# Key stacks moved with their zeros in 1 KB pieces, query rows in 512-byte pieces, and one wait fewer ahead of the stacks

## The reference, cut to what matters

```python
q = (layernorm(x) @ Wq.T + bq)          # 128 sequences, 64 tokens, 16 heads of 8
k, v = (ctx @ Wk.T + bk), (ctx @ Wv.T + bv)
scores = einsum('bhqd,bhkd->bhqk', q, k) / sqrt(8)
x = x + (softmax(scores) @ v) @ Wo.T + bo
z = layernorm(x)
# two gates: convolution over 4 channels, batch norm over all tokens, GELU, linear, softmax, top 32 of 128
x = x + (z @ W) * top32(gate_out) + (z * top32(gate_in)) @ W + bias
```

## Time and profile before

| | us |
|---|---|
| median of 3 runs | 524.53 |
| lowest, highest | 522.14, 526.05 |
| the profiled execution | 522.13 |
| its span | 520.3 |

### The profile page before, as it was taken

How to read it: one execution, slowest core, us unless ns; L and a number is a source line. 1 busy time by engine, 2 the same in 40 slices (tenths; PEclk the granted TensorE clock), 3 DMA queues, 4 the chain that set the end, 5 groups by cost and what they waited for, 6 DMA issues and landing times.

```text
span 520.3 us, 16344 instructions
## 1 busy us (share of the span) xinstructions
PE 414.4 (80%) x5516; PEld 314.0 (60%) x5516; DVE 408.7 (79%) x1940; ACT 391.4 (75%) x1061; POOL 363.5 (70%) x515
## 2 busy tenths in 40 slices
PE   3457999989999989999989564987787877777754
PEld 1125787868877858887777242765564645555543
DVE  7554478766777766767875359999999999999997
ACT  3414677867787858887667488899989898899893
POOL 7356667776777767876311023699989898999896
PEclk9997799988999999999999855578879698788687
DMA  5788788788788787788810000000000000000001
GB/s 159 157 211 196 159 197 196 197 204 195 172 183 184 191 195 176 161 185 182 178 47 7 1 0 2 1 21 23 21 22 37 12 36 22 21 21 22 23 21 40
DMA packets 138970, 53.02 MB, mean 102 GB/s; under 512 B 105146, under 2 KB 131195, under 8 KB 137339
## 3 DMA queue, kind: packets, MB, share of 16 engines
q1 hardware_dynamic: 136712, 51.47, 41.2%
q10 hardware_dynamic: 2176, 0.52, 0.5%
HBM read 34.67 MB, written 16.78 MB: 99 GB/s over the span
## 4 chain that ended last, share of the span: by engine, by line
DVE 37%; SPq 27%; PE 18%; DMA 7%; issue 4%; ACT 4%; POOL 2%; DVEq 0%; ACTq 0%; POOLq 0%
SPq L300 23%; DVE kst L1040 17%; DVE tops L1033 16%; DMA k_scratch<-k_parts 4%; PE ps_pv L360 4%; DMA qst<-q_scratch 3%; PE ps_col L345 2%; SPq L285 2%; PE ps_row L389 2%; PE ps_mix L375 1%; PE ps_proj L437 1%; SPq L247 1%; PE ps_proj L415 1%; PE ps_turn L430 1%; PE ps_mix L604 1%
## 5 line engine op out<-in xcount | busy, mean ns | idle before, releaser
L892 DVE TENSOR_REDUCE m<-ps_row 128x8 f32<-128x512 f32 x128 | 82.3, 686 | 57.1 <-PE ps_row L389 56.9
L650 ACT ACTIVATE pT<-ps_col 128x512 f32<-128x512 f32 x128 | 68.7, 589 | 29.1 <-PE ps_col L345 28.9
L1033 DVE MAX8 tops<-kst 128x8 f32<-128x128 f32 x384 | 78.1, 268 | 0.0
L360 PE MATMUL ps_pv<-vx,pT 128*64 128x18 f32 x2048 | 73.3, 214 | 0.0
L360 PEld LDWEIGHTS ps_pv<-vx,pT 128*64 128x64 f32 x2048 | 66.9, 141 | 7.1 <-issue 4.5
L1040 DVE MATCH_REPLACE8 kst<-tops,kst 128x128 f32<-128x128 f32 x264 | 69.0, 266 | 0.0
L389 PE MATMUL ps_row<-kst,qst 96*64 96x128 bf16 x1024 | 42.7, 228 | 7.8 <-DMA qst<-q_scratch 7.7
L345 PEld LDWEIGHTS ps_col<-qst,kst 100*128 100x128 bf16 x1024 | 35.0, 100 | 22.8 <-issue 11.9
L345 PE MATMUL ps_col<-qst,kst 100*128 100x64 bf16 x1024 | 42.8, 197 | 5.9 <-DMA qst<-mT 5.7
L553 PE MATMUL ps_proj<-wf_sb,x2T 128*128 128x128 f32 x128 | 25.6, 362 | 26.2 <-ACT x2T L821 26.2
L389 PEld LDWEIGHTS ps_row<-kst,qst 96*64 96x64 bf16 x1024 | 33.5, 116 | 11.8 <-DMA qst<-q_scratch 9.9
(11 more groups left out here) (156 smaller groups left out, 1213.3 us busy)
## 6 DMA issues: line engine op xcount, KB each, us to landing
k_scratch<-k_parts SPq DMA_DIRECT2D x32, 192.0 KB, 3.0
q_scratch<-q_parts SPq DMA_DIRECT2D x32, 192.0 KB, 3.1
kst<-k_scratch SPq DMA_DIRECT2D x32, 192.0 KB
qst<-q_scratch SPq DMA_DIRECT2D x32, 192.0 KB
xr<-in_x_dram SPq DMA_DIRECT2D x16, 256.0 KB, 4.3
cT<-in_ctxT_dram SPq DMA_DIRECT2D x16, 256.0 KB, 3.6
kst<-k_scratch SPq DMA_DIRECT2D x32, 128.0 KB
qst<-q_scratch SPq DMA_DIRECT2D x32, 128.0 KB
```

The lines of the kernel that those rows point to most:

```text
L360: mm = pe.matmul(pv_flat[pp * SEQ:(pp + 1) * SEQ, h * 2 * VW:(h + 1) * 2 * VW], pT[:, 2 * j + pp, hh, :], vx[s][:, 2 * hp + pp, h, :], sta ...
L650: act.activation(pT[:, b % PT_RING, :, :], ps_col[b % 2][:, :, :], ACT.Exp, scale=SCALE).then_inc(act_exp, 1)
L892: dve.tensor_reduce(m32[:, b // 4, :, 4 * j:4 * j + 4].rearrange("q a h -> q h a"), ps_row[b % 2][:, :, :, :], AX.X, ALU.max).then_inc(dve ...
L1033: ins = dve.max(tops[g % 2][:, n, 8 * rnd:8 * rnd + 8], source(g, rnd, n))
```

## The change

The key parts get a new home, `k_frames`: each part of a pair lies as 64 values of the sequence and 64 zeros. It is zeroed once by VectorE, and GpSimd writes only the places of the values. The parts go to DRAM with the zeros (pieces of 1 KB in place of 512 bytes), and come back so into the stack: a row is 16 pieces of 1 KB in place of 64 of 128 bytes. The three stack buffers are therefore no longer zeroed. In DRAM a row of either scratch tensor is followed by a gap of 32 values; by that a query row is 16 pieces of 512 bytes. The stacks' wait for `act_mT` is gone.

```diff
+GAP = 32
...
-        k_parts = sb("k_parts", [128, PARTS, GTOK], BF16)
+        k_frames = sb("k_frames", [128, 2 * (PARTS * GTOK + SEQ)], BF16)
...
-        q_scratch = [nc.dram_tensor(f"q_scratch{s}", (2, PARTS, 128, HALF), BF16).ap() for s in range(2)]
-        k_scratch = [nc.dram_tensor(f"k_scratch{s}", (2, PARTS, 128, HALF), BF16).ap() for s in range(2)]
+        q_scratch = [nc.dram_tensor(f"q_scratch{s}", (2, PARTS, 128, HALF + GAP), BF16).ap() for s in range(2)]
+        k_scratch = [nc.dram_tensor(f"k_scratch{s}", (2, PARTS, 128, GTOK + GAP), BF16).ap() for s in range(2)]
+        k_parts = [k_frames[:, :].rearrange("c (a x) -> c a x", a=2)[:, :, n * GTOK:(n + 1) * GTOK]
+                   .rearrange("c a (p m) -> c a p m", p=PAIRS)[:, :, :, 0:SEQ] for n in range(PARTS)]
...
             for s in range(STACKS):
-                if s == 1:
-                    sp.wait_ge(gp_zero, 1)
-                else:
-                    sp.wait_ge(dve_zero, s // 2 + 1)
-                if s == 2:
-                    load_x(2)
                 sp.dma_start(kst[s][MROWS:KROWS, :, :, :, :].rearrange("r h p a m -> r (h p a m)"), minus_rows).then_inc(rows_in, 16)
+            load_x(2)
...
+                for a in range(2):
+                    sp.dma_start(k_scratch[s][a, :, :, 0:GTOK].rearrange("n c t -> c n t"),
+                                 k_frames[:, a * PARTS * GTOK:(a + 1) * PARTS * GTOK].rearrange("c (n t) -> c n t", n=PARTS)
+                                 ).then_inc(k_out[s], 16)
...
-                        src = scratch[s][a, first:first + n].rearrange("n (i h) t -> (n i) (h t)", h=HEADS)
-                        rows = spread(a, n)
-                        dst = (kst[d][rows, :, :, a, :].rearrange("r h p m -> r (h p) m") if to_keys
-                               else qst[d][rows, :, :].rearrange("r h t -> r (h t)"))
-                        if to_keys:
-                            src = src.rearrange("r (x m) -> r x m", m=SEQ)
-                        sp.dma_start(dst, src).then_inc(moved[d], 16)
+                        src = scratch[s][a, first:first + n].rearrange("n (i h) t -> (n i) h t", h=HEADS)
+                        sp.dma_start(stacks[d][spread(a, n)], src[:, :, 0:stacks[d].shape[2]]).then_inc(moved[d], 16)
...
-                    wait(sp, act_mT, 2 * t)
                     wait(sp, pe_col, 8 * (t - 1))
...
-            dve.memset(kst[0][:, :, :, :, :].bitcast(F32).rearrange("r h p a m -> r (h p a m)"), 0.0).then_inc(dve_zero, 1)
+            dve.memset(k_frames[:, :].bitcast(F32), 0.0).then_inc(dve_zero, 1)
...
-                    dve.memset(kst[2][:, :, :, :, :].bitcast(F32).rearrange("r h p a m -> r (h p a m)"), 0.0).then_inc(dve_zero, 1)
...
-            pool.memset(kst[1][:, :, :, :, :].bitcast(F32).rearrange("r h p a m -> r (h p a m)"), 0.0).then_inc(gp_zero, 1)
```

More of the change, by code:

```diff
@@ L264, in _, with write_keys @@
             for s in range(STACKS):
[L266 to L271 removed]
                 sp.dma_start(kst[s][MROWS:KROWS, :, :, :, :].rearrange("r h p a m -> r (h p a m)"), minus_rows).then_inc(rows_in, 16)
[L274 removed]
+            load_x(2)
+            def write_keys(g):
                 s = g % 2
[L276 to L280, removed]
+                wait(sp, gp_split, 4 * g + 4)
@@ L281, in write_parts @@
                 if g >= 2:
-                    wait(sp, moved[slot(g - 2)], STACK * uses(g - 2))
+                    wait(sp, k_moved[slot(g - 2)], STACK * uses(g - 2))
                 for a in range(2):
-                    sp.dma_start(scratch[s][a].rearrange("n c t -> c n t"),
-                                 parts[:, :, a * HALF:(a + 1) * HALF]).then_inc(done[s], 16)
-            def stack(g, scratch, done, moved, to_keys):
+                    sp.dma_start(k_scratch[s][a, :, :, 0:GTOK].rearrange("n c t -> c n t"),
+                                 k_frames[:, a * PARTS * GTOK:(a + 1) * PARTS * GTOK].rearrange("c (n t) -> c n t", n=PARTS)
+                                 ).then_inc(k_out[s], 16)
@@ new lines, in write_queries, with stack @@
+            def write_queries(g):
+                s = g % 2
+                wait(sp, dve_split, 4 * min(g + 1, 2))
+                wait(sp, gp_qsplit, 4 * (g - 1))
+                if g >= 2:
+                    wait(sp, q_moved[slot(g - 2)], STACK * uses(g - 2))
+                for a in range(2):
+                    sp.dma_start(q_scratch[s][a, :, :, 0:HALF].rearrange("n c t -> c n t"),
+                                 q_parts[:, :, a * HALF:(a + 1) * HALF]).then_inc(q_out[s], 16)
+            def stack(g, scratch, out, moved, stacks, first_part):
@@ L302, in _ @@
+            kst_rows = [kst[s][:, :, :, :, :].rearrange("r h p a m -> r h (p a m)") for s in range(STACKS)]
+            qst_rows = [qst[s][:, :, :] for s in range(STACKS)]
             for t in range(FIRST, LAST + 1):
@@ L307, in _ @@
                 if there(t + 1):
-                    wait(sp, act_mT, 2 * t)
                     wait(sp, pe_col, 8 * (t - 1))
-                    stack(t + 1, k_scratch, k_out, k_moved, True)
-                    stack(t + 1, q_scratch, q_out, q_moved, False)
+                    stack(t + 1, k_scratch, k_out, k_moved, kst_rows, lambda n: PARTS - n)
+                    stack(t + 1, q_scratch, q_out, q_moved, qst_rows, lambda n: 0)
                 if there(t + 2):
-                    write_parts(t + 2, k_parts, k_scratch, k_out, k_moved)
-                    write_parts(t + 2, q_parts, q_scratch, q_out, q_moved)
+                    write_keys(t + 2)
+                    write_queries(t + 2)
             for g in range(GROUPS):
```

16 lines of the change are left out of this document (9 added, 7 removed).

## The result

| | us |
|---|---|
| before, median of 4 runs | 525.29 (522.14 to 531.24) |
| with the change, median of 4 runs | 602.07 (600.18 to 603.23) |
| ratio, 95% interval | 1.150 (1.145 to 1.155) |
| the profiled execution with the change | 602.0, its span 600.2 |

A forecast was written before the change was run, and what follows sets the result against it. Transfers were taken as the bound, TensorE 0.6 us below. Terms +1.6 + 1.0 + 0 - 0.8 - 0.1 = +1.7 us a cycle, 25.5 over 15 cycles, 24.5 with the start, on 522.1: 547 us, range 514 to 564.

The forecast's parts named there:

- the key stack: Its transfer with zeros, 1573 KB for 786, was to take 7.8 us for 6.2: +1.6 a cycle (-1.3 to +2.0).
- the removed wait: Dropping the stacks' wait for the maxima's copy was to give -0.1 us a cycle; maxima running beside stacks counted as nothing.
- the start: Before the first key stack: SP no longer waits 2.3 us for a memset; -1 us, once.
- stack ring: SP's closed cycle of stack issues, writes, loads and next key stack: from 15.23 to 16.9 us, 15 times.
- the upper bound: For the key stack's time: twice the query stack's 4.1 us for 786 KB, so 8.2 us.
- The gaps: Thin stretches of the DMA engines in a cycle, shortened by SP's quicker key issues: -0.8 us a cycle (-1.4 to 0).
- The writes: Key writes to DRAM double from 393 to 786 KB a group: +1.0 us a cycle (0.6 to 1.3).
- The query stack: Same bytes in 512-byte pieces instead of 8 KB: 0 us a cycle (-0.7 to +0.4).
- GpSimd's cover: Its split of the keys ends 6.9 us before their write, 4.5 with earlier SP, against 3.6 needed: free.
- The slow clock: Rival, chance 0.13: TensorE's standing still lowers its granted clock, cycle 17.6 us, total 557.
- Large pieces at an engine's rate: Rival, chance 0.21: key stack 6.0 us or less, TensorE bounds the cycle at 14.6 us, total 511.

The follow-up runs named there:

- e15: The whole change, with the maxima's transfer still sent (into rows no one reads) but not waited for; 584.3 us, 1.113 of before.
- e2: The kernel before without the stacks' wait for ACT's copy of the maxima, pieces as before; 520.6 us, ratio 1.003.
- e1: The changed kernel with the stacks' wait for ACT's copy of the maxima put back, nothing else; 587.9 us, 1.125 of before.
- e3: e1 with the gap behind query rows taken out, so a query row is one 8 KB piece; 607.0 us, 1.159 of before.
- e8: e1, key parts still written with their zeros, but stacks read only the values in 128-byte pieces; 542.3 us, 1.035 of before.
- e12: The kernel before with a 32-value gap behind each scratch row, so query rows come in 512-byte pieces; 525.9 us, ratio 1.003.
- e5: e1 with stack rows on neighbouring partitions instead of every fourth, same bytes and pieces; 690.4 us, 1.319 of before.
- e6: e1 with a gap of 128 values in place of 32 behind each DRAM row; 586.6 us, 1.121 of before.
- e7: e3 with the gap behind key rows taken out too, so a key row is one 16 KB piece; 591.8 us, 1.131 of before.

## Why the prediction was wrong, by its steps

Two steps failed: the price of the key stack was too low, and the removed wait was taken for free. The first is the larger and by itself leads out of the range, whose top was 564: with nobody waiting for the maxima (e15) the kernel still takes 584, some 4 of it the filling of rows. The 79.9 us between the spans are the forecast's 24.5, and four things that it had not:

| | us |
|---|---|
| forecast: 1.7 x 15 less 1 at the start | 24.5 |
| stack ring longer than forecast: e15's 18.47 against 16.93, x 15 | 23.1 |
| maxima in line, in the cycle: 19.77 - 18.47, x 15 | 19.5 |
| rest of the span after the last stack: 278.9 - 268.3 | 10.6 |
| start: +1.25 in place of -1 | 2.2 |

Of the 10.6 after the last stack, 3.1 are again the maxima's (275.8 in e15), which with the 19.5 are the 22.6 from above. Not all of that is the removal's: with the wait back the maxima still cost some 8.6.

**The removed wait: the step that failed outright.** "The small transfers of the maxima now run beside the stacks more often; with 512-byte pieces in the query stack I count that as nothing." They do not run beside the stacks, they stand behind them. The price was in how much SP had issued before. e15 shows that it is the whole cost of the removal. I did name the row that would grow, the 5.7 us of the earlier trace rows. What I missed: the 2.1 us of the wait were read in a kernel where SP came to the key stack after the second maxima by itself in most cycles (and e2 agrees, removing it there is free). With the rest of the change SP is ahead by 5.1 us, and there the wait is what keeps the maxima in front. A wait's total says what it costs in the kernel it was read from, not what it orders in the changed one.

**The key stack: mis-sized.** I took 7.8 us, from 7 to 8.2. It runs for 9.8 to 11 us from the first piece to the last, and the landing moved by 3.6 us where I had 1.6. The step that failed is the upper bound, twice the query stack's 4.1 us. First, the 4.1 is a window of one cycle that closes when the last pieces start. Measured as the 9.8 is, from the first piece to the end of the last, the query stack of the kernel before takes 4.7 us in that cycle and 4.9 as a mean of 14, and twice 4.9 is 9.8. Second, I used the pace of SP (3.97 us for six issues) only to go below the bound. In the records of pieces the query stack runs under a lighter load than the key stack of e1: 8 KB take 458 ns as a mean (the quickest some 308), 57 ns for 1 KB where the key pieces have 77, and the fullest engine is busy for some 3.7 of the 4.9 us where in e1 it is busy throughout. Why emptier engines and quicker pieces there, fuller engines and slower pieces here, come to twice the time is open: no run has the query stack's bytes doubled. The Trainium skill's rule of 512 bytes for line rate, "DMA: Bandwidth & Descriptors", section Specifications, would have made the stack faster in 1 KB pieces than in 128-byte ones for the same bytes. The runs agree that the smaller piece has a lower rate in an engine (128 bytes in 13 ns, 1 KB in 46 at the quickest), yet the stack with half the bytes in eight times smaller pieces is the quicker by a third.

**The gaps: -0.8 did not come.** SP did get free of the key issues 2.2 us sooner, and spent it in the query issues. The line of issued transfers has a length, so room gained by one is waited for by the next. In e3, with few query pieces, SP did come to the key write 3.1 us sooner than in e1 (8.8 after the stack's issue against 11.8), and the write landed 2.5 us later after its issue (9.2 against 6.7). The stack and the gap together were to be +0.8 us a cycle, and are 18.47 - 16.17 = +2.3 from e8 to e15.

**The writes: right.** +1.0 predicted, +0.94 (e8). **The query stack: right** in the kernel before (e12); beside the large key stack 512-byte rows are 19 us better than 8 KB ones (e1 and e3), which no term had. **GpSimd's cover: right for the keys**, whose split ends 2.5 us or more before SP issues the key write (0.4 for the first group). For the queries it is used up: I had half a microsecond of waiting there, and with the change SP waits 12.1 us for that split in eight groups. In e1 and e15 the split is done 0.8 us or more ahead, so I read it as following from the late maxima and not as a cost of its own.

**The rest after the last stack: left out.** I multiplied a cycle by 15 and stopped. With the change TensorE lags the stacks, so after the last key stack it still has a group behind it to finish. ACT issues the last maxima 25.8 us after the last key stack before, and 37.1 us after it with the change. In e15 this is 32.6.

**The start: wrong sign.** The first key write is issued at 12.1 in place of 14.3, but it lands at 24.7, since it is twice as large and stands behind all loads of the start. The first matmul on a stack comes at 40.8, not 36.0.

**The rivals.** The slow clock was half there: PEclk is 7 to 8 in many slices and 0.831 over the profiled run, against 0.872 before, but I read it as a result of TensorE's waits: e15 has a lower clock, 0.814, and is 18 us faster. Large pieces at an engine's rate, 6.0 us or less for the key stack, is what 128 pieces at the quickest 46 ns would give, 5.9 us. They do not get it.

## What to carry to other kernels

Before removing a wait, ask what it will keep in order on the queues once the rest of the change is in, not only how long it is waited for now: here it was free to remove in the kernel before and cost 14 us in the changed one, where it had kept a 16 KB transfer ahead of 1.5 MB. To put zeros into a transfer in order to have larger pieces, compare the number of pieces on the fullest engine times the time of one under load, and take that time from a transfer with the same spread over partitions and at full flow, over many cycles and with the same two ends. When a cycle grows, add what the slower engine owes after the last one.

## What the runs showed of the hardware

- A small transfer that ACT issued waited for what SP had issued before it, and for no more: in the kernel with the change 64 pieces of 256 bytes, issued at 203.14, all start within 0.7 us from 209.09, when 1,509 of 1,536 key pieces have started. Issued at 99.75, with 640 key pieces issued or being issued, they start after 651.
- The destination partitions alone can make a transfer 1.6 times as long: 15.8 against 9.8 us for the key stack in e5 and e1, with pieces of 1 KB taking 123 and 77 ns where the quickest take 44 to 46.
- Pieces of 128 bytes take 13 ns with hardly any spread in every kernel that has them, all on every fourth partition.
- 32 values or 128 behind a row, 1 KB or 16 KB in a piece: the key stack took 9.1 to 9.8 us as a mean (e1, e3, e6, e7), on the same partitions.
